# The first 256 tokens in plain fp32 products, and the first block's experts by halves

## The reference

```python
x = x + attn(_layernorm(x))
x = x + ffn(_layernorm(x))

def attn(x):                       # x: (1, 4096, 256)
    q, k, v = jnp.split(x @ w_qkv, 3, axis=-1)      # 16 heads of 16
    q, k = elu(rope(q) * SCALE) + 1.0, elu(rope(k) * SCALE) + 1.0
    # token after token: kv += k v^T, ks += k
    # out_t = (q @ kv) / max(q . ks, 1e-6)
    return out @ w_out

def ffn(x):
    weights = _routing_weights(x, Wr, temperature)  # (tokens, 8)
    gate = jnp.einsum('btd,edi->beti', x, Wg)       # 8 experts, 256 inner
    up = jnp.einsum('btd,edi->beti', x, Wu)
    e_out = jnp.einsum('beti,eid->betd', jax.nn.silu(gate) * up, Wd)
    return jnp.einsum('bte,betd->btd', weights, e_out)
```

## Time and profile before

| | |
|---|---|
| time, median of 3 runs | 808.24 us (808.12 to 808.8) |
| profiled execution: its span | 806.5 us (no other time is given for it) |
| TensorE busy | 760.2 us, 94% |
| VectorE, ScalarE, GpSimd busy | 603.2, 465.4, 484.7 us |
| first gate product on TensorE | 83.66 us |
| HBM read, written | 16.13 MB, 4.19 MB |

### The profile page before, as it was taken

One profiled execution on the slowest core, in us unless ns is written; L12 is line 12 of the kernel. 1 busy time (PEld: TensorE's weight loads), 2 busy tenths in 40 slices (PEclk: granted clock), 3 DMA queues, 4 the chain that ended last, 5 costly groups with the idle time before them and its releaser, 6 DMA issues.

```text
span 806.5 us, 18062 instructions
## 1 busy us (share of the span) xinstructions
PE 760.2 (94%) x6660; PEld 654.1 (81%) x6660; DVE 603.2 (75%) x1596; ACT 465.4 (58%) x886; POOL 484.7 (60%) x538
## 2 busy tenths in 40 slices
PE   4475899999999999999999999999999999999997
PEld 2364688888888888888888888888888888888886
DVE  6788797878877797778877797787877787765433
ACT  3664776666566656666666556657665566534221
POOL 3785678765666665655666666566666555653232
PEclk9676799999999999999999999999999999999999
DMA  4544124122211123122101221121111121100000
GB/s 139 127 103 110 41 78 93 40 43 68 40 28 24 34 66 41 41 43 54 41 20 35 43 66 40 41 43 27 41 40 40 41 53 28 27 1 27 1 1 27
DMA packets 97319, 38.27 MB, mean 47 GB/s; under 512 B 74192, under 2 KB 96976, under 8 KB 97232
## 3 DMA queue, kind: packets, MB, share of 16 engines
q1 hardware_dynamic: 90704, 30.83, 18.1%
q10 hardware_dynamic: 6528, 6.29, 2.7%
HBM read 16.13 MB, written 4.19 MB: 25 GB/s over the span
## 4 chain that ended last, share of the span: by engine, by line
PE 88%; DVE 5%; POOL 2%; ACT 2%; issue 1%; DMA 1%; SPq 0%; DVEq 0%; ACTq 0%; POOLq 0%
PE y L446 22%; PE gate L413 22%; PE up L413 21%; PE front L288 5%; PE back L333 3%; PE front L289 3%; PE back L369 2%; PE back L344 2%; PE up L381 1%; PE front L311 1%; PE front L394 1%; PE back L326 1%; PE back L356 1%; POOL a_lo L1131 1%; PE back L311 1%
## 5 line engine op out<-in xcount | busy, mean ns | idle before, releaser
L1159 POOL TENSOR_TENSOR h_lo<-work,h_hi 128x512 fp32r<-128x512 f32 x128 | 166.3, 1299 | 66.0 <-ACT h_hi L640 66.0
L1131 POOL TENSOR_TENSOR a_lo<-am,a_hi 128x512 f16<-128x512 f32 x120 | 144.6, 1206 | 54.9 <-ACT a_hi L568 52.3
L446 PE MATMUL y<-wd_hi,h_hi 128*128 128x256 f32 x512 | 148.1, 289 | 1.7 <-DVE xa L1032 1.7
L446 PE MATMUL y<-wd_lo,h_hi 128*128 128x256 f32 x512 | 143.9, 281 | 0.0
L446 PE MATMUL y<-wd_hi,h_lo 128*128 128x256 f32 x512 | 143.8, 281 | 0.0
L1020 DVE TENSOR_TENSOR work<-work,up 128x512 f32<-128x512 f32 x128 | 87.1, 680 | 72.1 <-PE up L413 71.7
L640 ACT ACTIVATE h_hi<-work 128x512 fp32r<-128x512 f32 x128 | 80.6, 630 | 64.5 <-DVE work L1020 39.4
L1032 DVE SCALAR_TENSOR_TENSOR xa<-y,wo,xa 128x256 f32<-128x256 f32 x256 | 113.5, 470 | 4.5 <-PE y L446 4.5
L446 PEld LDWEIGHTS y<-wd_hi,h_hi 128*128 128x128 f32 x512 | 96.5, 189 | 4.9 <-issue 2.1
L446 PEld LDWEIGHTS y<-wd_lo,h_hi 128*128 128x128 f32 x512 | 96.4, 188 | 3.1
L446 PEld LDWEIGHTS y<-wd_hi,h_lo 128*128 128x128 f32 x512 | 96.4, 188 | 0.0
(11 more groups left out here) (200 smaller groups left out, 1722.2 us busy)
## 6 DMA issues: line engine op xcount, KB each, us to landing
xr<-xT SPq DMA_DIRECT2D x32, 128.0 KB, 2.5
xa<-x SPq DMA_DIRECT2D x32, 128.0 KB, 2.7
out<-xa SPq DMA_DIRECT2D x32, 128.0 KB, 1.7
xa<-Wg ACTq DMA_DIRECT2D x8, 256.0 KB, 2.9
work<-Wd ACTq DMA_DIRECT2D x8, 256.0 KB, 2.9
work<-Wu ACTq DMA_DIRECT2D x8, 256.0 KB, 2.8
work<-w_qkv SPq DMA_DIRECT2D x2, 384.0 KB, 3.7
qT<-q_st SPq DMA_TRANSPOSE x32, 3.2
```

Source lines behind the costliest of these rows:

```text
L446: m = pe.matmul(Y[t // 2][:, t % 2 * D:(t % 2 + 1) * D], h_p[hi][:, n % 2, t * P:(t + 1) * P], wd_p[wi][:, u // KI, u % KI, :], start=(n % ...
L1131: pool.tensor_tensor(a_p[1][:, heads(r), :], am_place(g, r).rearrange("p (h n) -> p h n", h=4), a_p[0][:, heads(r), :], ALU.subtract).then ...
L1159: pool.tensor_tensor(h_p[1][:, n % 2, :], hb[:, n % 2, :], h_p[0][:, n % 2, :].bitcast(F32), ALU.subtract).then_inc(s_hlo, 1)
```

## The change

- **Tiles 0 and 1 (`exact(g)`) use plain fp32 operands.** The input is centred instead of the weights for them (`x_mean` on TensorE, `x_c` on VectorE), and their q, k, v come from the raw w_qkv (`qkv_exact`). Their masked scores aren't split: `av_exact` takes them from SBUF in fp32, with `v` in fp32 (`v32`), as 16 products of 17 columns. `o_sum` falls away (`norm` reads PSUM). `proj_exact` and the router of the first group use raw operands. The column mean and the splitting of w_qkv come after that, for tile 2 on.
- **The first block's experts go by halves.** `GROUPS` has 9 entries: two of two tiles, then seven of four. In block 0 a unit is one whole expert on 256 tokens: units 0 to 7 on tiles 0 and 1, in plain fp32 (`three_exact`, `down_exact`), units 8 to 15 on tiles 2 and 3, in three products (`three_pair`, `down_pair`). `h_hi` and `h_lo` aren't made for units 0 to 7. There are two routers in block 0.
- **Weights.** The ring is gone. Each slab is loaded straight to the place of its `lo` part, read there raw by units 0 to 7, and split in place: `slab_lo` of an expert waits for that expert's gate, up or down. All 24 loads are issued from ScalarE's list without a wait.
- **`tcos`** is a `tensor_tensor` with a broadcast `rstd1` instead of a `tensor_scalar`.
- **The head's list is new** on all five engines and reaches to step 9. From step 10 (unit 20) the loop is the one before, without the slab calls and with the router's number one higher.

```diff
+HF = 2
+PAIR = 2 * P
+GROUPS = ((0, 0, 2), (0, 2, 2)) + tuple((b, 0, NT) for b in range(1, NB))
+X2_AHEAD = {2: 3, 3: 5, 4: 7, 5: 10, 6: 12, 7: 14}
...
-        wg_p = [sb(f"wg_{s}", [P, E, KD, I], F32R) for s in ("hi", "lo")]
+        wg_lo_m, wg_raw = with_raw("wg_lo", "wg_raw", [P, E, KD, I])
+        wg_p = [sb("wg_hi", [P, E, KD, I], F32R), wg_lo_m]
...
+            def x_mean(g):
+                for k in range(KD):
+                    m = pe.matmul(BK[g][:, 0:P], mean_w[:, :], xr[:, g, k, :], start=(k == 0), stop=(k == KD - 1))
...
+            def qkv_exact(g):
+                w.wait_ge(s_xc, g + 1)
+                for k in range(KD):
+                    w.wait_ge(c_wqkv[k], 16)
+                    m = pe.matmul(qk_bank(g)[:, :], xr[:, g, k, :], wq_raw[:, k, 0:2 * D], start=(k == 0), stop=(k == KD - 1))
+                m.then_inc(s_qkv, 1)
+                w.wait_ge(s_v, g)
+                for k in range(KD):
+                    m = pe.matmul(R1[:, 0:D], xr[:, g, k, :], wq_raw[:, k, 2 * D:], start=(k == 0), stop=(k == KD - 1))
...
+            def av_exact(g):
...
+                for odd in range(2):
+                    for p in range(NP):
+                        r = 2 * (p // 4) + odd
+                        m = pe.matmul(BK[odd][:, p * W1:(p + 1) * W1], am_place(g, r)[:, p % 4 * P:(p % 4 + 1) * P],
+                                      v32[:, g, 2 * p + odd, :], start=(g == 0 and p == 0), stop=(p == NP - 1),
+                                      skip_group_check=True)
...
+            def three_exact(ps, weights, n):
+                for m_ in range(KI):
+                    for k in range(KD):
+                        m = pe.matmul(ps[:, m_ * PAIR:(m_ + 1) * PAIR],
+                                      weights[:, expert(n), k, m_ * P:(m_ + 1) * P],
+                                      x2_raw[:, 0, k, 0:PAIR], ...)
+
+            def three_pair(ps, weights, n):
+                for m_ in range(KI):
+                    for wi, xi in ((0, 0), (1, 0), (0, 1)):
+                        for k in range(KD):
+                            m = pe.matmul(ps[:, m_ * PAIR:(m_ + 1) * PAIR], weights[wi][:, expert(n), k, m_ * P:(m_ + 1) * P],
+                                          x2[xi][:, 0, k, PAIR:2 * PAIR], ...)
...
             def load_slab(n):
-                if n >= NSL:
-                    w.wait_ge(*slab_lo_done(n - NSL))
...
+                src, raw, _, e_ = slabs[n]
+                act.dma_start(raw[:, e_, :, :], src[e_].rearrange("(k p) n -> p k n", p=P)).then_inc(expert_in[e_], 16)
...
             def slab_lo(n):
                 w.wait_ge(s_slab_hi, n + 1)
+                w.wait_ge((s_gate, s_up, s_down)[n % 3], e_ + 1)
...
-                v.tensor_scalar(tcos[:, :], tabs[:, g // NT % 2, g % NT, 0:HALF], rstd1[:, g % NRS:g % NRS + 1], None, ALU.mult).then_inc(s_tcos, 1)
+                v.tensor_tensor(tcos[:, :], tabs[:, g // NT % 2, g % NT, 0:HALF],
+                                rstd1[:, g % NRS:g % NRS + 1].broadcast_to([P, HALF]), ALU.mult).then_inc(s_tcos, 1)
...
-            x_hi(0); load_slab(0); wqkv_hi(0); wqkv_hi(1)
+            load_slab(0); load_slab(2); load_slab(1); load_slab(3); load_slab(4); load_slab(5); load_slab(6)
...
-            load_wqkv(0); load_wqkv(1)
-            load_xr(0); load_xa(0); load_xr(1)
+            load_xr(0); load_wqkv(0); load_xr(1); load_wqkv(1); load_tab(0); load_xa(0); load_xa(1); load_small()
```

More of the change, by code:

```diff
@@ L459, in tensor_program @@
+            scores(8, 1); x2_T(7); down(13); up(14); logit_rows(2); up(15); logit(2); gate(16); qkv(9); gate(17)
+            down(14); up(16); av(8); up(17); down(15); o_T(8); state(8); gate(18); proj(8); up(18); down(16)
+            scores(9, 0); gate(19); x2_T(8); down(17); up(19); scores(9, 1)
+            for s in range(10, STEPS):
                 a, c, n = s, s - 1, NT * (s - LAG)
-                router = (s - LAG) // NT if (s - LAG) % NT == 0 else -1
+                router = (s - LAG) // NT + 1 if (s - LAG) % NT == 0 else -1
@@ new lines, in acc @@
+                w.wait_ge(s_route, routed(j, "wo"))
+                w.wait_ge(s_x2n, g + 1)
+                v.scalar_tensor_tensor(out=xs, in0=y, scalar=wo[:, b % 2, t0 + t, expert(n):expert(n) + 1], in1=xs,
+                                       op0=ALU.mult, op1=ALU.add).then_inc(s_acc, 1)
+            setup_first(); x_c(0); ones_vx(); bn(0); w_sum(); mean_var(0); x_c(1); var_eps(0); bn(1); mean_var(1)
+            tcos_scale(0); var_eps(1); cos(0); tcos_scale(1); rope(0); phi(0); rtemp_first(); wc(0); k_lo(0); q_lo(0)
@@ new lines, in vector_program @@
+            mean_var(7); tcos_scale(4); bn2(2); mask(3, 0); var_eps(7); mean_var2(2); var_eps2(2); mask(3, 1)
+            acc(0, 0); acc(0, 1); mask(3, 2); acc(1, 0); h_up(2); mask(3, 3); ln2(2); cos(4); wr_lo(); x2_lo(2)
+            rope(4); acc(1, 1); acc(2, 0); slab_lo(2); phi(4); h_up(3); o_sum(3, 0); o_sum(3, 1); den_max(3)
+            den_rec(3); norm(3); acc(2, 1); k_lo(4); q_lo(4); o_lo(3); slab_lo(5); st_add(3); x1_add(3); x_lo(5)
+            bn(8); bn2(3); mean_var(8); mean_var2(3); var_eps2(3); h_up(4); acc(3, 0); ln2(3); mask(4, 0); x2_lo(3)
@@ new lines, in vector_program @@
+            mask(4, 1); slab_lo(8); mask(4, 2); tcos_scale(5); acc(3, 1); route_sum(1); mask(4, 3); h_up(5)
+            slab_lo(11); bn(9); route_zone(1); var_eps(8); mean_var(9); slab_lo(14); o_sum(4, 0); cos(5); bn(10)
+            rope(5); o_sum(4, 1); den_max(4); var_eps(9); phi(5); route_nearest(1); den_rec(4); h_up(6); norm(4)
+            k_lo(5); q_lo(5); acc(4, 0); o_lo(4); mean_var(10); acc(4, 1); acc(5, 0); route_weight(1); st_add(4)
+            x1_add(4); bn2(4); x_lo(6); mean_var2(4); var_eps2(4); acc(5, 1); slab_lo(17); ln2(4); mask(5, 0)
@@ new lines, in vector_program @@
+            mask(5, 1); route_first(1); route_second(1); slab_lo(20); tcos_scale(6); x2_lo(4); mask(5, 2)
+            route_tie(1); mask(5, 3); cos(6); h_up(7); rope(6); route_ix2(1); acc(6, 0); route_s2(1); phi(6); h_up(8)
+            o_sum(5, 0); k_lo(6); o_sum(5, 1); tcos_scale(7); den_max(5); q_lo(6); den_rec(5); norm(5); x_lo(7)
+            h_up(9); o_lo(5); route_both(1); st_add(5); x1_add(5); bn2(5); mask(6, 0); mean_var2(5); mask(6, 1)
+            var_eps2(5); route_out(1); acc(6, 1); ln2(5); mask(6, 2); acc(7, 0); cos(7); x2_lo(5); acc(7, 1); rope(7)
@@ new lines, in vector_program @@
+            mask(6, 3); phi(7); acc(8, 0); h_up(10); q_lo(7); k_lo(7); o_sum(6, 0); o_sum(6, 1); den_max(6)
+            den_rec(6); norm(6); x_lo(8); st_add(6); h_up(11); o_lo(6); acc(8, 1); mask(7, 0); x1_add(6); mask(7, 1)
+            tcos_scale(8); bn2(6); mean_var2(6); slab_lo(23); var_eps2(6); mask(7, 2); ln2(6); acc(9, 0); mask(7, 3)
+            x2_lo(6); acc(9, 1); acc(10, 0); cos(8); rope(8); acc(10, 1); h_up(12); x_lo(9); phi(8); o_sum(7, 0)
+            o_sum(7, 1); den_max(7); den_rec(7); norm(7); q_lo(8); k_lo(8); h_up(13); o_lo(7); tcos_scale(9)
@@ new lines, in vector_program @@
+            acc(11, 0); acc(11, 1); acc(12, 0); x1_add(7); bn2(7); mean_var2(7); var_eps2(7); st_add(7); ln2(7)
+            acc(12, 1); mask(8, 0); x2_lo(7); mask(8, 1); h_up(14); acc(13, 0); mask(8, 2); route_sum(2)
+            route_zone(2); acc(13, 1); route_nearest(2); h_up(15); mask(8, 3); cos(9); x_lo(10); route_weight(2)
+            rope(9); var_eps(10); phi(9); h_up(16); o_sum(8, 0); o_sum(8, 1); den_max(8); den_rec(8); norm(8)
+            acc(14, 0); acc(14, 1); q_lo(9); h_up(17); o_lo(8); route_first(2); k_lo(9); acc(15, 0); acc(15, 1)
```

768 lines of the change are left out of this document (463 added, 305 removed).

## The result

The changed kernel takes 835.99 us (median of 4 runs, 832.02 to 837.86), the kernel before 808.18 beside it: ratio 1.034, 95% interval 1.032 to 1.037. Forecast were 801.7, with a range of 789 to 813. The profiled execution took 832.02 us; its span is 830.3, where the forecast had 800.0.

A forecast was written before the change was run, and what follows sets the result against it. TensorE's own work was taken to bound B and C, one tile's latency chain A; 55 (A) + 133.4 + 7 (B) + 604.6 (C) = 800.0, plus 1.7 gives 801.7 us, range 789 to 813.

The forecast's parts named there:

- Stretch A: Start to the first gate (expert) product, bound by the latency of one tile's chain through all engines; forecast 55 us, before 83.66.
- one price: Each record of the fp32 `av` of tiles 0 and 1 was taken at 0.14 us, 4.5 us a tile.
- my walk: Step-by-step timing of tiles 0 and 1 up to the first gate: scores at 26, x2_T at 48 and 54, gate at 55.
- Rival 2: Before the first gate: early expert loads hold up the transposes and w_qkv, +10.4 us, gate at 65.4, time 812; chance 0.12.
- Stretch B: First gate product to unit 20's gate, bound by TensorE's work; forecast 133.4 us of work plus 7 of waits, before 118.24.
- The waits in B I put at 7, not at 2.65: TensorE's idle time from first gate to unit 20's gate: 7 us because VectorE's load nearly equals TensorE's; bounds 2 to 20.
- rival 1: VectorE becomes the bound in the fp32 phase: waits 15 us instead of 7, time 809.7; chance 0.17.
- my count, 75 and 44 us: VectorE's work from tile 1's `nat` to unit 7's `acc`, 75 us against TensorE's 74; then 44 against 59.
- 2 x 6.3 us of TensorE: Attention of tiles 2 and 3, moved behind the first gate, priced at 6.3 us a tile, 12.6 in all.
- TensorE's own work: First gate to unit 20's gate: 112.8 plus 12.6 for tiles 2 and 3 plus 8 fp32 surcharge, 133.4 us.
- Stretch C: Unit 20's gate to the end: same instructions in both programs, so unchanged at 604.6 us.
- rival 3: The fp32 expert products' weight loads don't hide: 0.81 instead of 0.43 us for 96 products, +36, time 838; chance 0.05.

## Why the prediction was wrong, step by step

**Stretch A: mechanism right, 4.5 us short.** Gate at 59.5 for 55 (bounds 48 to 65; expected 52 to 58). TensorE in order of time:
```profile
24.20 0.26 PE L386 MATMUL gate<-qT,kT 64*128 64x128 f16 x1 [7.14 <-DMA qT<-q_st]
...
30.46 4.14 PE L409 MATMUL back<-v,am_raw 128*128 128x17 f32 x32
36.25 0.26 PE L386 MATMUL gate<-qT,kT 64*128 64x128 f16 x1 [1.66 <-DMA qT<-q_st]
...
42.30 1.89 PE L409 MATMUL back<-v,am 128*128 128x17 f32 x8
44.03 1.87 PE L409 MATMUL back<-v,hb 128*128 128x17 f32 x8
```
The qk copy came at 13.0 (forecast 12.5), scores at 24.2 (26), av of tile 0 took 4.1 (4.5), x2_T of tile 0 came at 49.2 (48). The av of tile 1 took 6.85 us instead of 4.5: 32 records from 42.30 to 49.15, 0.21 each, at a granted clock of 1.2 GHz. Tile 0's took 0.13 in the mean: 0.12 each up to 33.4 us, at 2.4 GHz, and 0.21 after that, at 1.2. So there is no one price, as I had it: 0.14 lies a little above the price at the higher clock, and 0.19, a whole fp32 load, fits neither. The Trainium skill (TensorE: Matmul & The Clock Gate, "Weight-path perf modes") has no fast weight load for fp32; the trace agrees in direction, 0.12 a record with 17 columns against 0.025 with 51 columns on 16-bit weights. This part also makes most of A's spread: in the three kernels with the gate at 61.2 or 61.3 all of tile 0's av ran at 1.2 GHz and took 6.84 us, in the others 3.8 to 4.5. Also in A at 1.2 GHz, and not in my walk: the fp32 router rows of tiles 0 and 1, 57.66 to 59.46. Rival 2 (early expert loads hold up the transposes of tiles 0 and 1) came in small: the qT of tile 1, issued at 30.27 among slab loads, took 5.8 us to land against 3.2 for tile 0's, and TensorE waited 1.66 us for it. It came once more in B, at tile 4.

**Stretch B, the failed step: "The waits in B I put at 7, not at 2.65".** They were 18.8, and the cause is the one of rival 1, which had 15 for them: VectorE becomes the bound. I had seen that its work equals TensorE's, and priced it at a few us of waiting; and I had counted too little of it. It was busy 139.2 of 161.1 us, my count, 75 and 44 us, together 119, was too low by 20. Where the work of B comes from can be read off the two traces. VectorE's records in it add up to 158.9 us, before to 114.1 (they overlap, so that it is busy 139.2 and 98.3). Of the 44.8 more, 28.8 are the attention of seven tiles for five, 9.8 the steps of three routers for two (24.3 us for 14.5: halving the tokens of a router didn't halve its cost), and 5.5 weight splits that were in A before; hb (0.68 us) and `acc` (0.47) take as long as they did. The count in the prediction isn't itemised, so which of these it had too low stays open. 5.6 us are what VectorE loses beside GpSimd's splits (the run without them), and nothing was put down for that. So the two tiles that I priced at 2 x 6.3 us of TensorE are 29 us of VectorE records, in a stretch where it was already busy 98 of 118 us.

**Stretch B, TensorE's own work: 142.3 for 133.4.** Start to start a fp32 unit took 44.9/8 = 5.6 us for 5.2, a half unit in three products 36.2/8 = 4.5 for 4.2; together 6 of the 8.9 us. For the fp32 units the price held and the clock did not: four products take 1.73 us at 2.4 GHz, so 5.2 a unit, and 2.4 to 3.1 where the clock was lower. After the idle time before 76.8, and again before 108.8, the granted clock fell to 1.2 GHz; with the first products of B that makes 8.1 us at half pace, some 4 us lost. Where TensorE waited less (the two runs without splits) its clock was 0.99 and it was busy 139.3 to 140.1. Such a cost of the waits themselves wasn't in the prediction.

**Stretch C: "so C is common: 604.6 us" was wrong by 5.2 us.** The instructions are common, the addresses are not: v32 moves x2 by 2,176 bytes. v32 behind all else gives 605.3.

**Edits priced at nothing.** The fp32 loads hide: 0.43 us a product at 2.4 GHz, start to start; rival 3 is out. `tcos` as a tensor form waits like the scalar form:
```profile
L953 DVE TENSOR_TENSOR tcos<-tabs,rstd x32: 155/672/1191, 13.1 to 711.1; 128x8 f32<-128x8 f32 x32
```
672 ns in the median for 8 columns, against 785; by the rule of the Trainium skill (SBUF — State Buffer, "Who interferes with whom") it had to wait too, and the trace agrees: the five that overlap nothing of GpSimd take 155 to 166 ns, and 26 of the other 27 end 18 to 28 ns after a GpSimd instruction does.

**The sum as it came out:** 59.47 + 142.29 + 18.77 + 609.77 = 830.30. What decides against the scheme, as an estimate from these rows: B can't be shorter than TensorE's 139 to 142 us of work. With the earliest gate seen (57.9) and C at 605.3 that is 802 to 805 us of span before any wait in B, against 806.5 before. All that the head's gain left over was 1 to 4 us, and TensorE waited 19 us in B, 12 even without any splits.

Of the 34 us between forecast and median 11.8 are the waits in B, 8.9 TensorE's work there, 5.2 the addresses, 4.5 stretch A, and 4 lie between the profiled execution and the median.
